# Convolution attention by query halves, with shared query rows copied on chip by GpSimd

## The chip, the cores and the metric

The kernel runs on one core of a Trainium2 chip. The metric is the device time of one launch in microseconds. The five engines of the core run their own instruction streams and wait for one another through semaphores: TensorE (PE in the profile), VectorE (DVE), ScalarE (ACT), GpSimd (POOL) and SyncE (SP). DMA transfers are issued from an engine's queue, here mostly SyncE's.

## The reference

The whole program is a convolution block with attention, then a self-attention and a mixture of experts. Only the attention beside the convolution matters here. Eight images of 32 x 32 positions, 8 heads of 8 channels:

```python
logits = jnp.einsum('bnid,bnjd->bnij', qf, kf)      # 1024 queries x 1024 keys per image and head
logits = logits + rel_w + rel_h                     # relative position terms in x and in y
weights = jax.nn.softmax(logits, axis=-1)
attn = jnp.einsum('bnij,bnjd->bnid', weights, vf)
```

## The kernel before

The function `attention` works on 16 groups (`NG`; an image and four of its heads, `HG`), each of 1024 tokens in 8 tiles of 128 (`TT`). The query operand `qf` holds, for each head and each half of the keys, a column per token and 120 rows: 64 for the relative logits in x (high and low parts), 32 for those in y (of the 16 image rows of that key half), 24 for the query channels in three parts. A 121st row (`ROW_M`) takes minus the maximum. The key operand `kf` holds one-hot rows against the relative logits, and the key channels. So one matmul over 120 or 121 rows gives complete logits. All rows but the 32 for y are the same for both key halves and are loaded twice.

Each group goes through two passes. The first pass finds the maxima: for each head and tile of 128 queries two matmuls (L664) write 128 x 1024 logits into one of two pairs of PSUM banks, `sm`, and VectorE reduces them (L644) to a column of `nmax`. For each pair of heads TensorE turns 16 such columns (L679, "turn"), VectorE casts them into `mrow` (L657), and SyncE sends them into row `ROW_M` of `qf` (`maxima`, L639, two DMAs per head). The second pass computes transposed scores, 128 keys by 512 queries, into two PSUM banks `st` (L907); ScalarE takes their exp into SBUF (L882, `probs`); TensorE multiplies by the values into `pv` (L922, `weighted`: four heads side by side in four column strips, two instructions each). ScalarE copies `pv` out (L874) and SyncE stores it (L832).

The passes are overlapped by groups: in a *period*, group n is in the second pass and group n+1 in the first, which runs four tiles ahead, so its last four tiles belong to group n+2. There are three sets of `qf`, `kf` and `va`; the third `qf` is `q_all`. In a period TensorE's order is written out: 16 double steps of two scores, one `weighted` group, two scores, and four first-pass matmuls. A score waits for the exp that frees its bank (`exp_done`). Exps and scores go by key tile, then head, then query half. The turns come at the first-pass tiles 12 and 28 of 32.

SyncE's order in a period: the loads of group n+2 (`load_queries`, L618, L620, L625, the values L820, the keys L631), once all of group n-1 is through; then the store of group n-1; then the DMAs of the maxima. Periods 1 to 12 are a hardware loop of three periods per turn. Beside this GpSimd splits the expert weights in 32 pieces (L853 to L864: load, cast, subtract, two stores), as fast as the DMAs allow.

Before the main block a start block computes the relative logits of the last four images (L783, L753, L765), stores them, loads groups 0 and 1 and makes the first pass of group 0.

## Time and profile before

| | |
|---|---|
| median of 3 runs | 2465.53 us (2460.08 to 2470.38) |
| profiled execution | 2465.86 us, span 2464.0 us, mean granted TensorE clock 0.934 |
| TensorE matmul busy | 2184.8 us (89%), 10534 instructions |
| VectorE busy | 1342.1 us (54%) |
| ScalarE busy | 1214.7 us (49%) |
| GpSimd busy | 272.7 us (11%) |
| DMA | 291.40 MB, mean 118 GB/s |
| first-pass reductions, L644 | 512, 604.0 us busy, 229.7 us idle before |
| exps, L882 | 1024, 556.6 us busy, 264.4 us idle before |

The span is that of the instructions on the slowest core; the execution's time is slightly longer. An engine's busy time is summed over its instructions. A matmul's end is modelled and matmuls overlap, so "busy" on TensorE does not mean that it runs at its peak. In a row of a timeline, the text in brackets tells how long the engine had been idle and what ended the wait; "x4" is four instructions merged into one row, whose duration runs from the first start to the last end.

### The profile page before, as it was taken

Reading aid. Unit: us, or ns where it says so; the run is one execution under the profiler, and the core shown is the slowest. Engines: PE = TensorE matmul, PEld = TensorE weight load, DVE = VectorE, ACT = ScalarE, POOL = GpSimd, SP = SyncE. Lnnn points to the kernel's source line nnn. Section 1 sums busy time; section 2 is a strip of 40 time slices with the busy share of each in tenths; the row PEclk is TensorE's granted clock in tenths of the full one; section 3 lists DMA queues with packets and bytes.
Section 4 is the critical chain, followed back from the end, with each engine's and each line's share of the span. In section 5 each row is a group of like instructions: output and inputs, shape, how many; then the busy total and the mean of one; then the engine's idle time right before and its main releaser. Section 6 shows DMA issues by size and latency. Waiting matters only on the chain. (4 is left out here: it accounts for less than half of the span.)

```text
span 2464.0 us, 32921 instructions
## 1 busy us (share of the span) xinstructions
PE 2184.8 (89%) x10534; PEld 1511.8 (61%) x10534; DVE 1342.1 (54%) x2054; ACT 1214.7 (49%) x2160; POOL 272.7 (11%) x258
## 2 busy tenths in 40 slices
PE   4999999946999999999999983888888893999997
PEld 3777888745545444454455431677777772888886
DVE  6232333124777667677777712466565652566665
ACT  2121222121467666667677771555555552566664
POOL 1000000000122222210000002212122200000000
PEclk9999999955699999999999996999999996999999
DMA  2322243396777678776567203322322114444531
GB/s 72 98 64 64 65 139 122 131 202 197 210 160 168 147 160 164 165 143 105 91 112 121 42 9 101 117 90 93 98 98 90 51 52 156 149 146 139 210 128 60
DMA packets 154696, 291.40 MB, mean 118 GB/s; under 512 B 32448, under 2 KB 94656, under 8 KB 150464
## 3 DMA queue, kind: packets, MB, share of 16 engines
q1 hardware_dynamic: 145568, 263.83, 41.6%
q0 software_dynamic: 7680, 25.17, 3.6%
q8 instruction: 75, 1.23, 0.2%
q10 hardware_dynamic: 1312, 0.67, 0.1%
q14 instruction: 61, 0.50, 0.1%
HBM read 179.69 MB, written 107.25 MB: 116 GB/s over the span
## 5 line engine op out<-in xcount | busy, mean ns | idle before, releaser
L644 DVE TENSOR_REDUCE a_nmax<-a_sm 128x1 f32<-128x1024 f32 x512 | 604.0, 1219 | 229.7 <-PE a_sm L664 229.5
L882 ACT ACTIVATE p_shared<-a_st 128x512 f32<-128x512 f32 x1024 | 556.6, 596 | 264.4 <-PE a_st L907 262.9
L922 PE MATMUL a_pv<-p_shared,a_va 128*32 128x512 f32 x2048 | 276.5, 613 | 0.9 <-ACT p_shared L882 0.9
L664 PE MATMUL a_sm<-a_kf,a_qf 120*128 120x512 f32 x704 | 218.7, 429 | 62.6 <-DMA a_kf<-kq_d 38.3
L907 PE MATMUL a_st<-a_qf,a_kf 121*128 121x512 f32 x704 | 257.5, 444 | 17.7 <-ACT p_shared L882 8.0
L907 PEld LDWEIGHTS a_st<-a_qf,a_kf 121*128 121x128 f32 x704 | 121.1, 192 | 220.4 <-ACT p_shared L882 198.3
L1797 PE MATMUL x_h_ps<-x_v_hi,x_w 128*128 128x512 f32 x512 | 180.8, 395 | 25.4 <-DVE x_v_lo L1738 25.4
L664 PEld LDWEIGHTS a_sm<-a_kf,a_qf 120*128 120x128 f32 x704 | 136.6, 204 | 100.7 <-issue 32.6
L1811 PE MATMUL x_y_ps<-x_h_hi,x_w 128*128 128x512 f32 x512 | 178.0, 389 | 0.0
L1748 DVE SCALAR_TENSOR_TENSOR x_h_lo<-x_hid,x_wts,x_h_hi 128x512 fp32r<-128x512 f32 x128 | 96.0, 750 | 138.0 <-ACT x_h_hi L1719 138.0
L1715 ACT ACTIVATE x_hid<-x_h_ps,x_b 128x512 f32<-128x512 f32 x128 | 88.4, 691 | 130.6 <-PE x_h_ps L1797 125.7
L1797 PEld LDWEIGHTS x_h_ps<-x_v_hi,x_w 128*128 128x128 f32 x512 | 97.1, 190 | 45.3 <-issue 25.5
L1382 PE MATMUL b_o_ps<-b_pT,b_v 128*128 128x256 f32 x512 | 120.7, 379 | 0.0
L1213 ACT ACTIVATE b_probs<-b_s_ps,b_nmax 128x1024 f32<-128x1024 f32 x64 | 71.3, 1113 | 95.9 <-DVE b_nmax L1303 95.9
L507 PE MATMUL c_acc<-c_y_hi,c_w_hi 128*128 128x512 f32 x288 | 117.6, 408 | 0.0
L507 PE MATMUL c_acc<-c_y_hi,c_w_hl 128*128 128x512 f32 x288 | 117.2, 407 | 0.0
L507 PE MATMUL c_acc<-c_y_lo,c_w_hi 128*128 128x512 f32 x288 | 117.1, 407 | 0.0
L507 PE MATMUL c_acc<-c_y_lo,c_w_hl 128*128 128x512 f32 x288 | 117.1, 407 | 0.0
L507 PE MATMUL c_acc<-c_y_hi,c_w_lo 128*128 128x512 f32 x288 | 117.1, 406 | 0.0
L1303 DVE TENSOR_REDUCE b_nmax<-b_s_ps 128x1 f32<-128x1024 f32 x64 | 78.4, 1224 | 69.7 <-PE b_s_ps L1367 62.9
L907 PE MATMUL a_st<-p_q_all,a_kf 121*128 121x512 f32 x320 | 112.5, 433 | 0.3 <-ACT p_shared L882 0.3
L1811 PEld LDWEIGHTS x_y_ps<-x_h_hi,x_w 128*128 128x128 f32 x512 | 96.1, 188 | 20.0
(248 smaller groups left out, 3615.2 us busy)
## 6 DMA issues: line engine op xcount, KB each, us to landing
x_w<-w_d SPq DMA_DIRECT2D x32, 1024.0 KB, 8.5
rel_d<-p_shared SPq DMA_DIRECT2D x12, 2048.0 KB, 12.2
a_qf<-rel_d SPq DMA_DIRECT2D x44, 512.0 KB
a_qf<-rel_d SPq DMA_DIRECT2D x44, 256.0 KB
p_q_all<-rel_d SPq DMA_DIRECT2D x20, 512.0 KB
a_qf<-kq_d SPq DMA_DIRECT2D x66, 128.0 KB
c_xtok<-in_x SPq DMA_DIRECT2D x8, 1024.0 KB, 5.7
va_d<-c_va SPq DMA_DIRECT2D x16, 512.0 KB, 4.8
```

The lines of the kernel that those rows point to most:

```text
L507: m = nc.tensor.matmul(image_rows(acc[u][:]), wt[:, k, :] if tap is None else wt[:, k, tap, :], y[s][:, k, rows + dy:rows + dy + H // 2, d ...
L644: nc.vector.tensor_reduce(nmax[:, h, t:t + 1], sm[k % 2][:], axis=AX.X, op=ALU.max, negate=True).then_inc(sm_read, 1)
L664: m = nc.tensor.matmul(sm[k % 2][:, cols], qf[j][0:ROW_M, h, half, t * P:(t + 1) * P], kf[j][0:ROW_M, h, cols], start=True, stop=True)
L882: nc.scalar.activation(probs[:, t % 2, h, half * HALF:(half + 1) * HALF], st[half][:], ACT.Exp).then_inc(exp_done, 1)
L907: nc.tensor.matmul(st[half][:], kf[j][0:ROW_M + 1, h, t * P:(t + 1) * P], qf[j][0:ROW_M + 1, h, 2 * t // TT, half * HALF:(half + 1) * HALF ...
L922: m = nc.tensor.matmul(pv[32 * h:32 * h + 32, cols], va[j][:, t, h, :], probs[:, t % 2, h, cols], start=t == 0, stop=t == TT - 1, skip_gro ...
L1303: nc.vector.tensor_reduce(nmax[:, k:k + 1], s_ps[:], axis=AX.X, op=ALU.max, negate=True).then_inc(max_ready, 1)
L1382: m = nc.tensor.matmul(o_ps[:], v_sb[s][:, t, :], pT[k % 2][:, t, :], start=t == 0, stop=t == TT - 1)
L1715: nc.scalar.activation(hid[k % GB][:], h_ps[k % 2][:], ACT.Gelu, bias=b1_sb[s][:, e, f:f + 1]).then_inc(hid_ready, 1)
L1748: nc.vector.scalar_tensor_tensor(h_lo[k % HB][:], hid[k % GB][:], wts[s][:, e:e + 1], bits(h_hi[k % HB][:]), ALU.mult, ALU.subtract).then_ ...
L1797: m = nc.tensor.matmul(h_ps[k % 2][:], w[s][:, e, c, part, tile(f)], v[s][:, c, half(j)], start=i == 0, stop=i == 3 * KC - 1)
L1811: m = nc.tensor.matmul(y_ps[j][c][:], w[s][:, e, 2 + f // 2, part, f % 2 * C + c * P:f % 2 * C + (c + 1) * P], h[k % HB][:], start=first a ...
```

## The change

The common rows of the queries (the x logits and the query channels, now rows 0 to 87) are loaded once per group, for key half 0; GpSimd copies them to key half 1 (`double_queries`). The y rows are still loaded per half, and lie last, before `ROW_M`. The first pass goes by halves of 512 keys in four single PSUM banks (`SB`), with a reduction per half and one minimum over the two for each pair of heads. The turns are placed after the second tile of the next head, not before its first. The second pass goes by query half first, then key tile, then head; `st` has three banks (`STB`), `pv` one bank that is copied out after each half, and `probs` four slots. TensorE's order in a period is eight batches by the string `ORDER`: s is a score, m a first-pass matmul, v a group of `weighted`. SyncE stores the second half of group n-1 ahead of the loads of group n+2, and issues the maxima of heads 0 and 1, the store of the first half, and the maxima of heads 2 and 3 after them. GpSimd handles two pieces of the expert weights per period, with the copy after the first load. The values are loaded in two DMAs.

```diff
-    ROW_W, ROW_H = (0, W), (2 * W, 2 * W + H // 2)
-    ROW_Q = 2 * W + H
-    ROW_M = ROW_Q + 3 * DH
+    ROW_W, ROW_Q = (0, W), 2 * W
+    ROW_H = (ROW_Q + 3 * DH, ROW_Q + 3 * DH + H // 2)
+    ROW_M = ROW_H[1] + H // 2
...
+        nmax_half = sb("a_nmax_half", [P, 2, HG, TT])
...
-        sm = [ctx.enter_context(nc.psum_tensor(f"a_sm{i}", [P, TOK], f32)) for i in range(2)]
+        SB = 4
+        sm = [ctx.enter_context(nc.psum_tensor(f"a_sm{i}", [P, HALF], f32)) for i in range(SB)]
...
+        DOUBLED = 2 + 3
+        VA_LOADS = 2
+        LOADS = 4 + 3 + VA_LOADS
...
-                if t == 0 and h % 2 == 0:
-                    units.append((step, "turn", 0, (h - 1) % HG, 0))
-                units.append((step, "logits", d, h, t))
-                step += 1
-            return units if whole else units + [(step, "turn", 0, HG - 1, 0)]
+                units.append((step, "logits", d, h, t, 0))
+                units.append((step + 1, "logits", d, h, t, 1))
+                if t == 1 and h % 2 == 0:
+                    units.append((step + 1, "turn", 0, (h - 1) % HG, 0, 0))
+                step += 2
+            return units if whole else units + [(step, "turn", 0, HG - 1, 0, 0)]
...
+        STEPS = 2 * TT * HG
+        NS = STEPS
+        STB = 3
+        SLOTS = 4
+        BATCH = 2 * HG
+        NB = NS // BATCH
+        ORDER = "mssmsmsvvsmsmmsmsm"
...
+            dst = bits(qf[j][:])
+            for part in range(2):
+                r = ROW_W[part]
+                sp.dma_start(dst[r:r + W, :, 0, :], rel_g[0, part]).then_inc(doubled_loaded[j], 16)
+            for row, qpart in enumerate((0, 0, 1)):
+                r = ROW_Q + DH * row
+                sp.dma_start(dst[r:r + DH, :, 0, :], kq_g[qpart, 1]).then_inc(doubled_loaded[j], 16)
             for part in range(2):
                 for half in range(2):
-                    dst = bits(qf[j][:])
-                    r = ROW_W[part]
-                    sp.dma_start(dst[r:r + W, :, half, :], rel_g[0, part]).then_inc(loaded[j], 16)
                     r = ROW_H[part]
                     sp.dma_start(dst[r:r + H // 2, :, half, :], rel_g[1, part, half * H // 2:(half + 1) * H // 2]
                                  ).then_inc(loaded[j], 16)
-            for row, qpart in enumerate((0, 0, 1)):
-                r = ROW_Q + DH * row
-                for half in range(2):
-                    sp.dma_start(bits(qf[j][:])[r:r + DH, :, half, :], kq_g[qpart, 1]).then_inc(loaded[j], 16)
+
+        def double_queries(pool, n, j):
+
+            pool.wait_ge(doubled_loaded[j], (n // BUFS + 1) * 16 * DOUBLED)
+            nc.gpsimd.tensor_copy(qf[j][0:ROW_H[0], :, 1, :], qf[j][0:ROW_H[0], :, 0, :]).then_inc(doubled, 1)
...
-        def logits_max(dve, before, k, h, t):
+        def logits_max(dve, before, k, h, t, half):
             dve.wait_ge(sm_done, before + k + 1)
-            nc.vector.tensor_reduce(nmax[:, h, t:t + 1], sm[k % 2][:], axis=AX.X, op=ALU.max, negate=True).then_inc(sm_read, 1)
+            nc.vector.tensor_reduce(nmax_half[:, half, h, t:t + 1], sm[k % SB][:], axis=AX.X, op=ALU.max, negate=True).then_inc(sm_read, 1)
+            if h % 2 and t == TT - 1 and half:
+                dve.drain()
+                nc.vector.tensor_tensor(nmax[:, h - 1:h + 1], nmax_half[:, 0, h - 1:h + 1], nmax_half[:, 1, h - 1:h + 1], ALU.min
+                                        ).then_inc(nmax_ready, 1)
...
+            if not (isinstance(before, int) and before + k < SB):
+                pe.wait_ge(sm_read, before + k + 1 - SB)
             cols = slice(half * HALF, (half + 1) * HALF)
-            m = nc.tensor.matmul(sm[k % 2][:, cols], qf[j][0:ROW_M, h, half, t * P:(t + 1) * P],
-                                 kf[j][0:ROW_M, h, cols], start=True, stop=True)
-            if half == 1:
-                m.then_inc(sm_done, 1)
-
-        def first_pass(pe, n, j, whole, s, half, va_after=0):
-
-            for k, (step, what, d, h, t) in enumerate(first_pass_of[whole]):
-                if step == s and what == "logits":
+            nc.tensor.matmul(sm[k % SB][:], qf[j][0:ROW_M, h, half, t * P:(t + 1) * P],
+                             kf[j][0:ROW_M, h, cols], start=True, stop=True).then_inc(sm_done, 1)
...
-        probs = bits(shared[:])
+        probs = bits(shared[:]).rearrange("p a h n -> p (a h n)").rearrange("p (t h n) -> p t h n", t=SLOTS, h=HG)
         out = sb("a_out", [P, TOK])
-        st = [ctx.enter_context(nc.psum_tensor(f"a_st{i}", [P, HALF], f32)) for i in range(2)]
-        pv = ctx.enter_context(nc.psum_tensor("a_pv", [P, TOK], f32))
+        st = [ctx.enter_context(nc.psum_tensor(f"a_st{i}", [P, HALF], f32)) for i in range(STB)]
+        pv = ctx.enter_context(nc.psum_tensor("a_pv", [P, HALF], f32))
...
                 def period(n, j, more, ahead):
+                    if not (isinstance(n, int) and n == 0):
+                        store(n - 1, 1)
                     if ahead:
                         load(n + 2, (j + 2) % BUFS)
-                    if not (isinstance(n, int) and n == 0):
-                        store(n - 1)
                     if more:
-                        maxima(sp, n + 1, (j + 1) % BUFS, ahead)
-
-                def store(n):
-                    sp.wait_ge(out_ready, n * 2 + 4)
-                    sp.dma_start(att_d.rearrange("b g p n -> (b g) p n")[n], out[:]).then_inc(out_stored, 16)
-
-                sp.sem_inc(out_stored, 16)
+                        maxima(sp, n + 1, (j + 1) % BUFS, ahead, 0)
+                    store(n, 0)
+                    if more:
+                        maxima(sp, n + 1, (j + 1) % BUFS, ahead, 2)
...
+                for n in range(NG):
+                    load_weights(2 * n)
+                    if n + 2 < NG:
+                        double_queries(pool, n + 2, (n + 2) % BUFS)
+                    split_weights(2 * n)
+                    load_weights(2 * n + 1)
+                    split_weights(2 * n + 1)
...
                     for u in range(NS):
-                        t, h, half = u // (2 * HG), u // 2 % HG, u % 2
                         act.wait_ge(st_done, n * NS + u + 1)
-                        if h == half == 0:
-                            act.wait_ge(pv_done, n * 2 * TT + 2 * t + 2)
-                        nc.scalar.activation(probs[:, t % 2, h, half * HALF:(half + 1) * HALF], st[half][:], ACT.Exp
-                                             ).then_inc(exp_done, 1)
-                        if u in (3, 7) and not (isinstance(n, int) and n == 0):
-                            copy_out(n - 1, u // 4)
+                        if u % BATCH == 0:
+                            act.wait_ge(pv_done, n * 2 * TT + 2 * (u // BATCH) + 2)
+                        nc.scalar.activation(probs[:, u // HG % SLOTS, u % HG], st[(j + u) % STB][:], ACT.Exp).then_inc(exp_done, 1)
+                        if u == BATCH - 1 and not (isinstance(n, int) and n == 0):
+                            copy_out(n - 1, 1)
+                        if u == NS // 2 + BATCH - 1:
+                            copy_out(n, 0)
...
+                def weighted(n, j, w):
+
+                    half, t = w // TT, w % TT
+                    pe.wait_ge(exp_done, n * NS + HG * (w + 1) + STB)
+                    if w == 0:
                         pe.wait_ge(loaded[j], times_loaded(n, j))
                     if t == 0:
-                        pe.wait_ge(out_ready, n * 2 + half + 1)
-                    cols = slice(half * HALF, (half + 1) * HALF)
+                        pe.wait_ge(out_ready, n * 2 + half + 2)
...
                 def period(n, j, more, ahead):
-                    for s in range(0, STEPS, 2):
-                        t, h = s // HG, s % HG
-                        for half in range(2):
-                            scores(n, j, s, half)
-                        if t:
-                            weighted(n, j, t - 1, h // 2)
-                        elif not (isinstance(n, int) and n == 0):
-                            weighted(n - 1, (j - 1) % BUFS, TT - 1, h // 2)
-                        for half in range(2):
-                            scores(n, j, s + 1, half)
-                        if more:
-                            for step in (s, s + 1):
-                                for half in range(2):
-                                    first_pass(pe, n + 1, (j + 1) % BUFS, ahead, step, half)
-
-                pe.sem_inc(exp_done, 2)
+                    for i in range(NB):
+                        place = dict.fromkeys("smv", 0)
+                        for what in ORDER:
+                            k = place[what]
+                            place[what] += 1
+                            if what == "s":
+                                scores(n, j, i * BATCH + k)
+                            elif what == "m" and more:
+                                first_pass(pe, n + 1, (j + 1) % BUFS, ahead, i * BATCH + k)
+                            elif what == "v" and i:
+                                weighted(n, j, 2 * (i - 1) + k)
+                            elif what == "v" and not (isinstance(n, int) and n == 0):
+                                weighted(n - 1, (j - 1) % BUFS, 2 * (NB - 1) + k)
```

`scores`, the start block and the waits of the other engines follow the new counts. A score waits for `exp_done` at `n * NS + u + 1`, which starts at 3, that is for the exp three scores back.

## Rows read from the trace of the kernel before

**Rows 1.** Windows view: us, busy by engine (instructions), clock, DMA share, GB/s
```profile
494.00:646.00 152.00, 90.14 (x330) 77.04 (x330) 72.54 (x74) 29.76 (x36) 5.28 (x8) 0.50 0.74 193
646.00:1483.00 837.00, 806.46 (x4054) 394.00 (x4054) 568.81 (x506) 570.48 (x1057) 116.58 (x160) 0.98 0.63 126
```

**Rows 2.** Timeline, one double step: start us, us, engine, line, count, [idle before]
```profile
927.45 0.73 PE L907 MATMUL a_st<-p_q_all,a_kf 121*128 121x512 f32 x2
...
927.99 1.09 ACT L882 ACTIVATE p_shared<-a_st 128x512 f32<-128x512 f32 x2 [0.53 <-PE a_st L907]
928.02 1.09 PE L664 MATMUL a_sm<-a_kf,a_qf 120*128 120x512 f32 x4
928.69 2.36 DVE L644 TENSOR_REDUCE a_nmax<-a_sm 128x1 f32<-128x1024 f32 x2 [0.74 <-PE a_sm L664]
...
928.95 0.68 PE L907 MATMUL a_st<-p_q_all,a_kf 121*128 121x512 f32 x2
929.13 0.19 PEld L907 LDWEIGHTS a_st<-p_q_all,a_kf 121*128 121x128 f32 x1 [0.22 <-ACT p_shared L882]
...
929.56 1.06 PE L922 MATMUL a_pv<-p_shared,a_va 128*32 128x512 f32 x8
...
930.56 0.73 PE L907 MATMUL a_st<-p_q_all,a_kf 121*128 121x512 f32 x2
```

**Rows 3.** Timeline in the last group, which has no first pass
```profile
1441.26 0.73 PE L907 MATMUL a_st<-a_qf,a_kf 121*128 121x512 f32 x2
...
1444.36 0.73 PE L907 MATMUL a_st<-a_qf,a_kf 121*128 121x512 f32 x2
...
1480.10 1.92 PE L922 MATMUL a_pv<-p_shared,a_va 128*32 128x512 f32 x16 [0.94 <-ACT p_shared L882]
```

**Rows 4.** Timeline of VectorE, casts of the maxima
```profile
669.23 0.28 DVE L657 CAST a_mrow<-a_sm 16x128 fp32r<-16x128 f32 x1 [0.45 <-PE a_sm L679]
...
1351.35 0.28 DVE L657 CAST a_mrow<-a_sm 16x128 fp32r<-16x128 f32 x1 [0.45 <-PE a_sm L679]
...
1401.59 0.28 DVE L657 CAST a_mrow<-a_sm 16x128 fp32r<-16x128 f32 x1 [0.45 <-PE a_sm L679]
```

**Rows 5.** Timeline around a load wait and the loop's return
```profile
847.74 1.21 PE L664 MATMUL a_sm<-a_kf,p_q_all 120*128 120x512 f32 x4 [1.43 <-DMA a_kf<-kq_d]
...
855.25 1.22 PE L907 MATMUL a_st<-a_qf,a_kf 121*128 121x512 f32 x2 [3.25 <-issue]
...
856.40 1.94 PE L922 MATMUL a_pv<-p_shared,a_va 128*32 128x512 f32 x8
...
864.89 1.06 PE L922 MATMUL a_pv<-p_shared,a_va 128*32 128x512 f32 x8
```

**Rows 6.** Timeline, DMA issues: first load of a group; four maxima
```profile
805.14 0.68 SPq L618 DMA_DIRECT2D p_q_all<-rel_d  x1
...
904.73 2.69 SPq L639 DMA_DIRECT2D p_q_all<-a_mrow  x4
```

**Rows 7.** Waits view, 650 to 1480: us in total, times, longest
```profile
PE a_sm L664 <- DMA a_kf<-kq_d: 11.3, 6, 3.5
```

**Rows 8.** Timeline of VectorE in the start of the phase
```profile
545.30 1.22 DVE L644 TENSOR_REDUCE a_nmax<-a_sm 128x1 f32<-128x1024 f32 x1 [29.17 <-PE a_sm L664]
547.53 0.69 DVE L765 TENSOR_TENSOR p_shared<-a_rel,p_shared 128x512 fp32r<-128x512 f32 x1 [1.01 <-ACT p_shared L753]
```

**Rows 9.** View of DMA issues: count, KB each, median us to landing
```profile
kq_d<-c_kq_hi SPq DMA_DIRECT2D x32, 128.0 KB, 2.1
...
att_d<-a_out SPq DMA_DIRECT2D x1, 512.0 KB, 4.0
...
c_cb<-in_L_conv_conv_b SPq DMA_DIRECT2D x1, 0.5 KB, 5.2
```

**Rows 10.** Timeline of GpSimd
```profile
906.01 0.61 POOL L859 CAST p_bd_hi<-a_w_st 128x512 fp32r<-128x512 f32 x1 [16.69 <-DMA a_w_st<-in_L_ffn_W]
```

**Rows 11.** Waits view, 494 to 646
```profile
ACT a_hl L753 <- DMA rel_d<-a_hl: 25.7, 1, 25.7
```

157 lines of the change are left out of this document (87 added, 70 removed).

## The prediction

> **What bounds the kernel now.** I read the busy times by stage first. In the query/key attention stage (646 to 1483 us) TensorE counts as busy nearly throughout and VectorE and ScalarE for two thirds; in the start of the phase (494 to 646) TensorE runs at half clock while the DMA engines move 193 GB/s [rows 1]. "Busy" is weak here, since matmuls overlap, so I read the order of time next. A double step takes 3.11 us: two score matmuls (to the next start 0.57), four first-pass matmuls (0.93), two scores (0.61; a weight load is held 0.22 by an exp), one group of eight P·V matmuls (1.00) [rows 2]. Then the next scores start. The last group is the test, since it has no first pass: there the four first-pass matmuls are gone, and a double step still takes 3.10 us (1441.26 to 1444.36) [rows 3]. So the bound is not TensorE's work but a ring: score, exp on one of only two score banks, second score pair held until the exps free the banks, P·V behind them in TensorE's order, and only then the next scores: 0.54 to the first exp, 1.09 for two exps, about 0.48 to the P·V start, 0.99 for it, 3.10 in all.
>
> A period (one group, 16 double steps, two turns of the maxima) undisturbed is 50.24 us (casts at 1351.35 and 1401.59); over the 14 periods from 669.23 the mean is 52.3, so 29.0 us are lost in them [rows 4]. I see two causes. One is a load that arrives late: TensorE idles 1.43 us at 847.74 for keys whose group's loads began at 805.14 [rows 5, 6]; six such waits sum to 11.3 us [rows 7]. The other has no releaser and comes at the period where the hardware loop of three periods returns (three times): scores start at 855.25 after 3.25 us, and the next P·V group takes 1.94 us in place of 1.06, which is TensorE at half clock (1.2 of 2.4 GHz). From the first-pass matmuls at 847.74 to the P·V group at 864.89 lie 17.15 us where 0.93+0.61 and three double steps make 10.87, so one return costs up to 6.3 us [rows 5].
>
> **Part by part.**
> *Score banks 2 to 3, first-pass banks two of 1024 to four of 512, P·V by query halves, fixed order over 8 scores, 8 first-pass matmuls, 2 P·V groups.* The number of matmuls of each kind stays. The ring opens: at "mssmsmsvvsmsmmsmsm" score u needs the exp of score u-3. I walk one batch with 0.23 us per score or first-pass matmul (0.93 for four), 0.39 from a score's matmul to its exp, 0.545 per exp: the third score follows without a wait, the fourth (1.3 us in) needs the first exp (1.16), the four after P·V find free banks, and the eight exps end 0.6 us into the next batch, whose first scores need only exps 6 to 8. TensorE therefore becomes its own bound: two half batches of 0.57+0.93+0.45 each are 3.90 (0.45 is two scores at 0.225 with no exp to wait for); two P·V groups in a row take 0.86+1.00 (sixteen last 1.92 with the last one's own tail [rows 3], eight 1.06 [rows 2]), and one of two load exposures after P·V goes (0.12). That is 5.64; the walk with 0.225 per matmul gives 5.45; I take 5.6, 44.8 us for eight batches. Add two transposes (0.5 with their loads) and two places where the copy out of P·V delays an exp by 0.5 of which 0.3 reaches TensorE: 45.9.
>
> *Maxima by halves.* 64 reductions of 512 replace 32 of 1024. Two of 1024 last 2.36 us [rows 2], a single one 1.22 [rows 8], so the second starts 1.14 after the first. A VectorE operation of 512 columns from PSUM lasts 0.69 [rows 8]; from the 1024 form, less 512 columns at 1.04 ns, I also get 0.69. If successive ones overlap as now, their spacing is 0.69 less 0.08, 0.61: 4.9 us per batch, under TensorE's 5.6; without overlap 5.5, just under. Four banks hold 2.4 us of reductions through the P·V pair. The two minima and two casts of a period are under 0.3 each [rows 4]. I count 0.
> The Trainium skill, page "VectorE: DVE Perf Modes", section "The TRN2 errata", says an instruction pays a fixed term (about 150 cycles measured for one copy) and so speaks against halving tiles; charged fully, 64 reductions take an estimated 44 us per period, which is the third rival below.
>
> *The second turn of the maxima gets later.* Now its casts come four of 32 tiles before the end and scores of heads 2 and 3 are needed 3.1 us into the next period. After the change the transpose stands behind first-pass matmul 59 of 64, 3.9 us into the last batch; VectorE finishes that tile's reduction at 4.7, the cast at 5.0, and SyncE then issues four DMAs of the maxima in 2.69 us [rows 6]. The next period (from 5.75) wants heads 0, 1, 2, 3 in its first four scores, head 2 at 6.6 and head 3 at 7.1. With a landing 2.1 us after issue (the fastest small store [rows 9]), head 2 is there at 7.7 and head 3 at 9.0. So 2.0 us of new wait per period, in front of P·V and everything behind on TensorE. Bounds: 0 if landing is faster than any row shows; 4.0 (a store on an idle queue) gives 3.9; 5.2 (a 0.5 KB load at the start) gives 5.1 [rows 9]. I take 2.1: nothing else should be in the queue by then. Period: 45.9+2.1 = 48.0, against 50.2.
> The Trainium skill, "DMA: Bandwidth & Descriptors", section "Anatomy of one DMA", gives about 2.0 us fixed cost, most of it the write receipt; by it the wait is the same 2 us, and it also says a small size does not shorten it, which speaks against this edit. No row shows the landing of a maxima DMA itself.
>
> *Loads.* Per group now 4.63 MB (8 of 512 or 256 KB, six and three of 128 KB, values 512 KB); afterwards 3.25 MB. At 4.63 MB in the 42.6 us from 805.14 to 847.74 [rows 5, 6] (109 GB/s with the expert weights beside) 3.25 MB take 30 us. But SyncE now first waits for the copy out of the second half, at the end of the first batch and behind the new wait, so loads begin about 9 us into the period, not 3.5. Landing 39 to 41, needed at 42.4 (last batch): in time by 1 to 3 us. The weights go at two pieces per period, not some 3.5, which lightens the queue; their last pieces still end within the last period, hidden. The waits of 11.3 us go, with the half clock behind them: of the 29.0 us I leave 16 for three loop returns (5.3 each) and drop 13.
>
> *The copy on GpSimd.* 88 partitions by 4096. A 512-column cast there lasts 0.61 us [rows 10], so at most 8 x 0.61 = 4.9 us. Its inputs are loaded first (1.38 MB, 13 us), so it ends about 27 us into the period of 48: hidden by 15 us; the split of weights queued behind it is nobody's wait in this phase. Cost 0; if it were 20 us the first pass would wait.
>
> *Last group.* Without first pass a batch is 0.45+0.45 for the scores before the P·V pair, 1.86, 0.9, plus where ScalarE idles across the pair: by the walk 5.3, 42.4 against 49.6.
>
> *Start of the phase.* ScalarE waits 25.7 us for a store of relative logits [rows 11] that stands in SyncE's queue behind the loads of groups 0 and 1. These shrink by 2.75 MB; at 193 GB/s [rows 1] 14 us. Reductions of half size cost about 0.1 us more per 1024 columns where VectorE leads (33 of them, 3 us). Net 11; from 0 to 18.
>
> **Sum.** Before: 15 x 50.2 + 49.6 + 29.0 + about 4 for the first period = 836, which is the stage. After: 15 x 48.0 + 42.4 + 16 + 4 = 782. Gain 54, plus 11: 65. The profiled execution took 2465.86 us for a span of 2464.0 and lies on the median 2465.53: 2401, say 2400. What follows the phase is unchanged.
>
> **Rivals.**
> A, the wait for maxima isn't there (landing under 1 us, or slack in the ring hides it): period 46, 15 x 2.1 = 31 less, 2370. Speaks for it: no row shows these landings. Against: every landing read is 2 us or more. Chance 0.15.
> B, VectorE leads: no overlap of 512 reductions; in the stretch where seven first-pass matmuls come within 3 us the fourth bank is freed 0.3 us late, each batch: 8 x 0.25 = 2 us per period, 2430. Against: the pair of 2.36. Chance 0.14.
> C, loads later than their use, because they begin 5.5 us later in the period: 3 us of wait and clock loss in 15 periods, 45: 2445. Chance 0.08.
> D, slower: the maxima land 5.2 us after issue, as the small load did. The wait is then 5.1 us in two pieces, and TensorE falls to half clock after them, as at 855; that P·V group alone lost 0.88, a return 3 us beyond its idle time. Period 45.9+5.1+3 = 54.0: 15 x 3.8 = 57 more, less 7 (last group), 13 and 11: 2490. It decides from about 6.4 us of loss per period. Against: the queue is empty then. Chance 0.06.
> E, the exchange is neutral (ring gain eaten by a wait of 5 us): 2460. Chance 0.04.
>
> **Numbers.** Forecast 2400 with 0.53. Under 0.5% (12 us) a measurement of this kernel cannot tell from no change. The range runs from A's 2370 less the early loads' 10 to C's 2445: 2360 to 2445. Faster 0.53+0.15+0.14+0.06 of C = 0.88; same 0.05 (E and part of C); slower 0.07 (D and part of C).
>
> **What would show it.** The double step's two-bank ring gone: ScalarE waiting in other places, batch starts 5.6 us apart (5.4 to 5.7). Cast to cast of one kind 48 us. A wait of scores for the maxima once a period, 2 us. The two VectorE reductions 1.22 to 1.3 us per pair. No first-pass wait on loads of keys. The stage 646 to 1483 shortened to 782; the start from 152 to 141. It would be wrong if batches took over 5.9 us, or if the wait at the period's start passed 4 us.

## The result

The changed kernel takes 2449.1 us (median of 19 runs, 2436.7 to 2462.4) beside 2467.2 for the kernel before on the same chips (19 runs): a ratio of 0.9923, 95% interval 0.9906 to 0.9939. That is 18 us faster where 65 were forecast, and 4 us above the range. The profiled execution has a span of 2444.8 us (before 2464.0).

The two stages of [rows 1], in the windows view of the changed kernel:

```profile
494.00:646.00 152.00, 108.75 (x409) 89.05 (x410) 87.61 (x133) 43.06 (x60) 13.26 (x11) 0.54 0.78 204
646.00:1483.00 837.00, 771.08 (x3977) 402.75 (x3975) 583.07 (x993) 548.04 (x1035) 166.50 (x176) 0.97 0.59 100
```

In the start TensorE gets 409 matmuls done by 646 us instead of 330: work begins earlier (that window already holds some of the first period's matmuls in the changed kernel). To see the main stage apart from that, I use the casts of the maxima as the clock, as in [rows 4]. The same cast stands 17.9 us earlier than there, at 651.35 for 669.23, and 14 periods later at 1386.89:

```profile
651.35 0.27 DVE L681 CAST a_mrow<-a_sm 16x128 fp32r<-16x128 f32 x1
...
704.73 0.27 DVE L681 CAST a_mrow<-a_sm 16x128 fp32r<-16x128 f32 x1
...
754.96 0.27 DVE L681 CAST a_mrow<-a_sm 16x128 fp32r<-16x128 f32 x1
...
1386.89 0.27 DVE L681 CAST a_mrow<-a_sm 16x128 fp32r<-16x128 f32 x1
```

So the mean period is 735.54/14 = 52.5 us, 0.2 more than the 52.3 of before, and the least one (704.73 to 754.96) is 50.2, what it was. From that last cast to the last P·V the changed kernel takes 77.0 us, before 79.8. So the 18 us are the start's: the 14 periods lose 3 us and the last group gains 3. The forecast had periods of 48.0 and some 16 us of loss in 14 of them, 49.1 in the mean. It is the 3.4 us a period between 49.1 and 52.5 that has to be found.

One batch (8 scores, 8 first-pass matmuls, 16 P·V matmuls) in TensorE's timeline of the changed kernel:

```profile
713.63 0.50 PE L955 MATMUL a_st<-a_qf,a_kf 121*128 121x512 f32 x1
714.07 1.92 PE L968 MATMUL a_pv<-p_shared,a_va 128*32 128x512 f32 x16
715.92 0.51 PE L955 MATMUL a_st<-a_qf,a_kf 121*128 121x512 f32 x1
716.26 0.39 PE L688 MATMUL a_sm<-a_kf,p_q_all 120*128 120x512 f32 x1
716.50 0.40 PE L955 MATMUL a_st<-a_qf,a_kf 121*128 121x512 f32 x1
...
719.57 0.47 PE L955 MATMUL a_st<-a_qf,a_kf 121*128 121x512 f32 x1
719.97 1.93 PE L968 MATMUL a_pv<-p_shared,a_va 128*32 128x512 f32 x16
```

P·V starts at 714.07 and 719.97: 5.90 us, for the forecast's 5.6. No row has idle time in brackets (the view prints none below 0.15 us), so the batch is mainly TensorE's own stream. But the ring of [rows 2] is not fully open. The last score's weight load and the exps beside it:

```profile
718.89 2.07 ACT L930 ACTIVATE p_shared<-a_st 128x512 f32<-128x512 f32 x4 [0.18 <-PE a_st L955]
...
719.54 0.19 PEld L955 LDWEIGHTS a_st<-a_qf,a_kf 121*128 121x128 f32 x1
```

The first of these four exps ends at 719.49, 0.60 us after its start, and it is the one three scores back: the weight load of the last score before P·V begins 0.05 us behind it, 0.12 us after the load before it ended. In 103 of the 117 batches between 650 and 1420 us this weight load begins 0.05 us after that exp. Single matmuls start 0.23 us apart (716.26 to 716.50), the first one after P·V takes 0.34 and the last score before it 0.40. VectorE does its eight reductions behind it with a pause left, and at the end of a period this happens:

```profile
716.70 4.88 DVE L663 TENSOR_REDUCE a_nmax_half<-a_sm 128x1 f32<-128x512 f32 x8 [1.23 <-PE a_sm L688]
...
728.00 0.56 POOL L907 DMA_DIRECT2D w_d<-p_bd_hi  x1 [0.30 <-POOL p_bd_lo L904]
...
728.29 0.27 PE L705 MATMUL a_sm<-a_ident,a_nmax 128*16 128x128 f32 x1
...
729.09 0.54 POOL L893 DMA_DIRECT2D a_w_st<-in_L_ffn_W  x1
729.11 0.27 DVE L681 CAST a_mrow<-a_sm 16x128 fp32r<-16x128 f32 x1
...
729.40 2.70 SPq L658 DMA_DIRECT2D p_q_all<-a_mrow  x4
...
732.93 0.47 PE L955 MATMUL a_st<-p_q_all,a_kf 121*128 121x512 f32 x1 [1.32 <-DMA p_q_all<-a_mrow]
```

Eight reductions take 4.88 us (0.60 apart), under the 5.90. The transpose of the second turn at 728.29 leads to a cast at 729.11 and four DMAs of the maxima from 729.40; the scores that need them start at 732.93 after 1.32 us of waiting. Beside them stand two rows of GpSimd's queue at the same moment (its store of a weight half at 728.00 and its next load at 729.09): these matter below.

The longest waits of TensorE in the stage (columns: us in total, times, longest):

```profile
PE a_st L955 <- DMA a_qf<-a_mrow: 12.2, 8, 2.6
PE a_sm L688 <- issue: 10.8, 3, 3.7
PE a_st L955 <- DMA p_q_all<-a_mrow: 7.3, 5, 1.9
PE a_sm L688 <- DVE a_nmax_half L663: 6.8, 30, 0.9
PE a_sm L688 <- DMA a_kf<-kq_d: 4.0, 4, 1.4
```

The maxima are now waited for, 19.5 us in 13 waits at 11 places; the keys still, 4.0 in place of 11.3 [rows 7]; and the loop's three returns ("issue", 10.8). TensorE ran at half clock for some 3 to 5 us after all three returns and after four of the eleven places (near 681, 784, 1049 and 1262), and after none of the four waits for keys. The wait of 1.58 us at 783.41 and the return at 837.13, each with the P·V pair behind it (1.92 us otherwise) and the clock of the stretch:

```profile
783.41 0.47 PE L955 MATMUL a_st<-a_qf,a_kf 121*128 121x512 f32 x1 [1.58 <-DMA a_qf<-a_mrow]
...
785.13 3.17 PE L968 MATMUL a_pv<-p_shared,a_va 128*32 128x512 f32 x16
...
837.13 0.79 PE L688 MATMUL a_sm<-a_kf,p_q_all 120*128 120x512 f32 x1 [3.65 <-issue]
...
840.41 2.84 PE L968 MATMUL a_pv<-p_shared,a_va 128*32 128x512 f32 x16
```

```profile
785.00:789.00 4.00, 4.00 (x20) 1.27 (x20) 0.00 (x0) 0.82 (x2) 0.00 (x0) 0.66 0.01 2
837.00:842.00 5.00, 4.87 (x15) 2.62 (x19) 2.08 (x3) 2.28 (x4) 0.00 (x0) 0.50 0.03 7
```

Granted clock 0.66 and 0.50. SyncE's part of a period, in its timeline:

```profile
739.13 0.38 SPq L871 DMA_DIRECT2D att_d<-a_out  x1
739.81 1.47 SPq L631 DMA_DIRECT2D a_qf<-rel_d  x2
...
746.98 1.15 SPq L650 DMA_DIRECT2D a_kf<-kq_d  x3
```

The loads begin at 739.81, directly behind the store of the second half at 739.13, as forecast: 9 us into the period, whose first score starts at 730.75.

### The profile page after: what moved, and what is told of

The parts are those of the page before. It is cut to its first block and busy times, and to the rows that moved or that the text cites. A ratio compares the mean times of both kernels' runs of the same rounds, so it can differ in the third digit from the quotient of the medians.

```text
span 2444.8 us, 34315 instructions
## 1 busy us (share of the span) xinstructions
PE 2167.8 (89%) x10534; PEld 1531.7 (63%) x10534; DVE 1370.7 (56%) x2598; ACT 1204.2 (49%) x2160; POOL 329.9 (13%) x274
## 5 line engine op out<-in xcount | busy, mean ns | idle before, releaser
L663 DVE TENSOR_REDUCE a_nmax_half<-a_sm 128x1 f32<-128x512 f32 x1024 | 633.4, 682 | 204.6 <-PE a_sm L688 204.2
L930 ACT ACTIVATE p_shared<-a_st 128x512 f32<-128x512 f32 x1024 | 547.0, 604 | 275.8 <-PE a_st L955 266.6
L688 PE MATMUL a_sm<-a_kf,a_qf 120*128 120x512 f32 x704 | 277.9, 438 | 48.7 <-DMA a_kf<-kq_d 27.8
L955 PE MATMUL a_st<-a_qf,a_kf 121*128 121x512 f32 x704 | 288.4, 433 | 16.0 <-DMA a_qf<-a_mrow 12.2
L968 PE MATMUL a_pv<-p_shared,a_va 128*32 128x512 f32 x2048 | 258.0, 623 | 0.0
L955 PEld LDWEIGHTS a_st<-a_qf,a_kf 121*128 121x128 f32 x704 | 135.0, 193 | 142.3 <-ACT p_shared L930 100.5
L955 PE MATMUL a_st<-p_q_all,a_kf 121*128 121x512 f32 x320 | 128.8, 424 | 7.9 <-DMA p_q_all<-a_mrow 7.3
L688 PE MATMUL a_sm<-a_kf,p_q_all 120*128 120x512 f32 x320 | 121.1, 410 | 14.3 <-issue 10.8
L968 PEld LDWEIGHTS a_pv<-p_shared,a_va 128*32 128x32 f32 x2048 | 54.8, 112 | 116.4 <-issue 89.2
```

Source lines behind the costliest of these rows:

```text
L663: nc.vector.tensor_reduce(nmax_half[:, half, h, t:t + 1], sm[k % SB][:], axis=AX.X, op=ALU.max, negate=True).then_inc(sm_read, 1)
L688: nc.tensor.matmul(sm[k % SB][:], qf[j][0:ROW_M, h, half, t * P:(t + 1) * P], kf[j][0:ROW_M, h, cols], start=True, stop=True).then_inc(sm_ ...
L930: nc.scalar.activation(probs[:, u // HG % SLOTS, u % HG], st[(j + u) % STB][:], ACT.Exp).then_inc(exp_done, 1)
L955: nc.tensor.matmul(st[(j + u) % STB][:], kf[j][0:ROW_M + 1, h, t * P:(t + 1) * P], qf[j][0:ROW_M + 1, h, 2 * t // TT, half * HALF:(half + ...
L968: m = nc.tensor.matmul(pv[32 * h:32 * h + 32, :], va[j][:, t, h, :], probs[:, w % SLOTS, h], start=t == 0, stop=t == TT - 1, skip_group_ch ...
```

## The experiments

The theory at the start: the smaller load and the rearrangement by halves are two changes, the first gives what is gained, and the second exchanges the ring for TensorE's stream plus waits. Rivals were VectorE as the bound (B), the maxima's wait, and late loads (C).

**1. The smaller load and the copy alone,** in the kernel before: its order, two score banks and its P·V stay. The weights go at two pieces a period, as in the changed kernel.

```
 # kernel before, with load_queries, double_queries and the
+# weights' two pieces per period of the changed kernel
-        ROW_W, ROW_H = (0, W), (2 * W, 2 * W + H // 2)
+        ROW_W, ROW_Q = (0, W), 2 * W
```

> The kernel before with the loads alone changed: common query rows loaded once and copied by GpSimd, expert weights two pieces per period; both passes and their order stay as before. Theory 1 (the rearrangement by halves is worth nothing by itself, all of the gain is the smaller load): the start of the phase gets 18 us shorter, as in the changed kernel (block start 646 to 628), and the key waits of the first pass (11.3 us plus half clock) go: 2467 - 18 - 13 = 2436, below the changed kernel's 2449. Theory 2 (the rearrangement brings most of it): only the start gains, period mean stays 52.3: 2449 or above.

2437.95 us, ratio 0.9871 (0.9843 to 0.9899) against the kernel before: faster than the whole change. Its first cast of a period stands at 651.73, where the changed kernel has it too, so the start's gain comes with this part. No wait of TensorE for keys is left, and the mean period is 51.5: 50.1 to 50.5, and 55.1 to 56.4 at the three returns. No run separates the smaller load from the slower weights in the periods; for the start, run 2 does, which has these weights with the full load.

**2. The rearrangement alone:** the changed kernel, with both halves of the rows loaded.

```
-                sp.dma_start(dst[r:r + W, :, 0, :], ...).then_inc(doubled_loaded[j], 16)
+                for half in range(2):
+                    sp.dma_start(dst[r:r + W, :, half, :], ...).then_inc(loaded[j], 16)
```

> The changed kernel, but with both key halves' query rows loaded from memory again (19 DMAs less one, no copy on GpSimd). Theory 1: the start's 18 us are lost, and with 4.63 MB beginning some 9 us into the period instead of 3.5 the keys arrive late in every period: 2449 + 18 + 3 to 6 us in each of 13 periods = 2500 to 2540, slower than before. Theory 2: the load has slack, 2467.

2680.88 us, ratio 1.085 (1.0821 to 1.0879). The direction was right, the size far off: 15 us a period in the mean (67.5 for 52.5) where 3 to 6 were expected. The first cast stands at 676.44, 25 us later than with the smaller load, so the start's gain is not the weights'. The waits view has the cause:

```profile
PE a_sm L683 <- DMA a_kf<-kq_d: 188.4, 14, 16.2
```

188 us, up to 16.2 each. Without the smaller load the loads are the bound; the forecast had not asked what the new order does by itself. That the loads have become so close a bound made me look at them again after the next two.

**3. The maxima of key half 0 first,** each half with a semaphore of its own, so that the first four scores wait only for their half.

```
+            for half in range(2):
+                for h in (first, first + 1):
+                    ... .then_inc(max_loaded[half][h], 16)
```

> The changed kernel; of the four DMAs of maxima per turn, the two rows of key half 0 go first and have semaphores of their own, so that the first four scores of a period wait for two issues and not four (1.35 us less of 2.69). Theory 1 (the late maxima, and the half clock that the wait brings in some periods, eat the gain): the 1.3 to 1.9 us waits before the third score shrink to 0.6 at most, the waits of scores for the maxima rows fall from 19.5 us in total to under 6, and two or three half-clock stretches of 3.4 us go: 2449 - 14 - 8 = 2427 (2420 to 2435). Theory 2 (TensorE's batch of 5.90 us is all, the wait is hidden by VectorE's or ScalarE's lag): 2445 to 2449.

2454.72 us (2448 to 2470), ratio to the kernel before 0.9936 (0.9917 to 0.9955), beside 0.9923 for the changed kernel: no gain, mean period 52.8. The waits for the maxima fell from 19.5 to 15.3 us, those for keys rose from 4.0 to 10.3 and the returns from 10.8 to 13.5. Expected were waits under 6 us, so the run did not take them away, and it says only that sending key half 0 first is no cure.

**4. Reductions over 256 of the 512 columns** (half of the maxima's columns is left out), which takes load from VectorE only.

```
-            ... sm[k % SB][:], axis=AX.X, op=ALU.max, negate=True)
+            ... sm[k % SB][:, 0:256], axis=AX.X, op=ALU.max, negate=True)
```

> The changed kernel with every first-pass reduction over 256 of its 512 columns (the maximum of the other half is left out; the softmax is shifted by another number). VectorE's eight reductions per batch fall from 4.88 to some 2.7 us. Theory 1 (TensorE's issue bounds the batch): batches stay at 5.9 less at most 0.05, only the turn's 0.6 us bubble goes, about 1 us a period: 2435. Rival B of the prediction (VectorE holds the first-pass banks): batches fall to 5.6 or below, 2410.

2448.46 us, one run. A clean batch still takes 5.88 us, for 5.90: VectorE is not what holds the stage, and rival B, which expected 0.25 to 0.3 us a batch, is out. The waits view says where the time went instead:

```profile
PE a_sm L688 <- DMA a_kf<-kq_d: 18.6, 11, 7.5
...
PE a_sm L688 <- DVE a_nmax_half L663: 0.8, 2, 0.6
```

TensorE's waits for reductions went from 6.8 to 0.8 us, and those for keys from 4.0 to 18.6. In runs 3 and 4 alike, what is shortened in front comes back as a wait for keys: the loads are a second bound just behind the first.

**5. The loads ahead of the store.** Both wait for the last P·V of the group before; the store also for the copy out.

```
-                    if not (isinstance(n, int) and n == 0):
-                        store(n - 1, 1)
                     if ahead:
                         load(n + 2, (j + 2) % BUFS)
+                    if not (isinstance(n, int) and n == 0):
+                        store(n - 1, 1)
```

> The changed kernel with SyncE's loads for the group after next put ahead of its store of the second half. Both wait for the same P.V (ends near 735.7 in the period that begins at 731); the store also waits for the copy-out behind the batch's exponentials, so the loads start near 736 instead of 739.8. Theory 1 (late loads are a second bound that takes back what the TensorE stream gives): no first-pass waits for keys are left (4.0 us in the changed kernel), fewer windows at half clock, and the mean period falls from 52.5 towards 51.5; 2430 to 2442. Theory 2 (the loads land in time but for a few, the losses are turn, maxima and loop returns): within 0.3% of the changed kernel, 2442 to 2456. Theory 3 (contention): loads that begin while the maxima land delay the scores, 2455 or more.

2429.91 us (4 runs), ratio 0.9844 (0.981 to 0.9877): some 19 us less than the changed kernel (by the two medians, and by the two ratios), by two lines moved. Its SyncE and its waits:

```profile
725.71 2.69 SPq L658 DMA_DIRECT2D p_q_all<-a_mrow  x4
732.19 1.47 SPq L631 DMA_DIRECT2D a_qf<-rel_d  x2
...
740.77 0.39 SPq L871 DMA_DIRECT2D att_d<-a_out  x1
```

```profile
PE a_sm L688 <- issue: 9.0, 3, 3.4
PE a_st L955 <- DMA a_qf<-a_mrow: 6.4, 7, 1.2
...
PE a_st L955 <- DMA p_q_all<-a_mrow: 3.6, 6, 0.7
```

The loads start 6.5 us behind the issue of the maxima (725.71), not 10.4 (729.40 to 739.81). No wait for keys is left. The waits for the maxima fell too, from 19.5 to 10.0 us. None of them is followed by half clock here. Mean period 51.1; outside the returns 50.0 to 50.8. Theory 1 holds, and 1.4 us of the missing 3.4 is found: in 15 periods some 9.5 us of waits for the maxima, 4 for keys, 2 at the returns, and the four stretches at half clock, each 1.3 us or more (an estimate from the P·V pair at 785.13, 3.17 us for 1.92).

**6. Still earlier: rows at the scores' end,** only the values behind P·V.

```
+                    if late:
+                        sp.wait_ge(st_done, (n - 2) * NS)
                     load_queries(sp, n, j)
```

> As the run before, but query and key rows are loaded as soon as the last score of the group that held the buffers is done (near 732 in that period, 7.6 us earlier than in the changed kernel), and only the values wait for P.V. Theory 1: keys are never late and the DMA engines have the whole period; mean period 50.5 to 51.5, 2418 to 2438. Theory 2: within 0.3% of the changed kernel. Theory 3: the row loads queue up with the four maxima DMAs (2.7 us from cast to landing): if these are still under way at the scores' end they take longer, the maxima waits grow from 1.3 us a period, 2455 or more.

2446.08 us, ratio 0.9912 (0.9881 to 0.9942): the gain of run 5 is gone. The timelines of VectorE and GpSimd give a reason that neither theory had:

```profile
749.23 3.60 POOL L644 CAST a_qf<-a_qf 88x4096 fp32r<-88x4096 f32 x1 [28.16 <-DMA a_qf<-kq_d]
...
750.66 2.20 DVE L666 TENSOR_TENSOR a_nmax<-a_nmax_half 128x16 f32<-128x16 f32 x1
...
752.78 2.47 DVE L663 TENSOR_REDUCE a_nmax_half<-a_sm 128x1 f32<-128x512 f32 x4
```

The minimum of the two half maxima, 0.18 us otherwise, starts at 750.66 and ends within 0.05 us of GpSimd's copy (749.23 + 3.60 = 752.83). The longest of the 32 took 3.36 us, and each of the nine that took over 0.2 us ends some 0.03 us after the copy does. The earlier rows had moved the copy onto the minimum, and the turn behind it waited.

**7. The same with the copy in four pieces,** one for each head.

```
-            nc.gpsimd.tensor_copy(qf[j][0:ROW_H[0], :, 1, :], qf[j][0:ROW_H[0], :, 0, :])
+            for h in range(HG):
+                last = nc.gpsimd.tensor_copy(qf[j][0:ROW_H[0], h, 1, :], qf[j][0:ROW_H[0], h, 0, :])
```

> The kernel that loads the rows at the scores' end, with GpSimd's copy cut into four, one for each head. In that kernel VectorE's 128x16 minimum, 0.18 us otherwise, took 2.20 us at 750.66 and ended when GpSimd's 3.60 us copy (from 749.23) did, and up to 3.36 us elsewhere; the turn behind it waited. Theory 1 (the long copy holds VectorE's SBUF-to-SBUF operation, and that is why the earliest loads gained nothing): with pieces of 0.9 us the minimum takes at most some 1.1 us, the waits of the turn for VectorE (6.2 us) and half the periods above 52 go; 2420 to 2435. Rival (the early loads cost by their DMA traffic beside the maxima, and the minimum is a bystander): 2440 to 2450 as before.

2434.72 us, ratio 0.9849 (0.9817 to 0.9882): 11 us back (16 by the ratios, whose intervals just touch), and the turn's waits for reductions, 6.2 us in run 6, no longer stand in the view. The longest minimum is now 1.04 us, as long as a piece. The overlap is shown by the rows; its price of 11 us is likely from this run, and not measured closely. It is no better than run 5, since the maxima are waited for 12.6 us.

**8. First pass six tiles ahead,** on run 6.

```
-        AHEAD = TT // 2
+        AHEAD = 6
```

> The run before with the first pass six query tiles ahead instead of four: the last turn comes four logits matmuls (about 1.5 us of the stream) earlier, so the maxima land before the scores want them; the next keys are wanted 1.5 us earlier too. Theory 1: with the loads early this is free, the 1.3 us wait at each group's start goes, and the half clock behind it: 15 to 25 us below b2, 2400 to 2418, and the period is the batches' 47.2 plus turn and copies, 48.5 to 50. Rival (the least period of 50.2 has another cause than the maxima, such as the 5.90 us batches being stretched by copies and turns): same as b2.

2439.41 us, ratio 0.9881 (0.9852 to 0.991). The waits for the maxima are gone altogether, as expected, but of the 15 to 25 us only 7 came: TensorE waits for VectorE's reductions 24.0 us instead (7.3 in run 6), and the periods with a return are 57.4 to 58.2.

**9. Two score banks** in the changed kernel.

```
-        STB = 3
+        STB = 2
 # scores and exps take bank u % STB in place of (j + u) % STB
```

> The changed kernel with two score banks in place of three (the first pass keeps four banks). If the rearranged order is what takes the ring of score, exponential and score out of the way, nothing changes: 2445 to 2455. If the third bank does it, the batch goes from 5.90 to the ring's 6.20 to 6.22 (two double steps of 3.10 to 3.11 in the kernel before): 8 x 15 x 0.31 = 37 us, 2475 to 2490.

2491.2 us, ratio 1.009 (1.0062 to 1.0119). P·V to P·V:

```profile
717.55 1.92 PE L968 MATMUL a_pv<-p_shared,a_va 128*32 128x512 f32 x16
...
723.97 1.93 PE L968 MATMUL a_pv<-p_shared,a_va 128*32 128x512 f32 x16
```

6.42 us, a little over the ring's 6.20, and a mean period of 54.8. So without the third bank the ring is the bound again; the new order on two banks is worse than the old.

**10. A first pass of 256 columns** on run 5 (matmuls and reductions; a part of the maxima is left out).

```
-            nc.tensor.matmul(sm[k % SB][:], qf[j][0:ROW_M, ...
+            nc.tensor.matmul(sm[k % SB][:, 0:256], qf[j][0:ROW_M, ...
```

> The kernel with the loads ahead of the store, with the first pass's matmuls and reductions over 256 of the 512 keys of a half (a part of the maxima is left out). Theory: TensorE's stream is what sets the batch, so it falls from 5.90 us by eight first-pass matmuls of half the columns (8 x 0.107 = 0.85 us) to about 5.1 to 5.3 unless ScalarE's eight exponentials of 0.53 us with their hand-over bound it first; main stage 15 x 8 x 0.6 = 70 us shorter, 2350 to 2370. If the loads bound the period from behind (11 DMA-engine seconds of 0.63 x 50 us = 32 us of full use a period), the gain shows as waits for keys instead.

2398.04 us, one run; a miss of 30 us. Clean batches fell to 5.43 us (P·V at 686.59 and 692.02 in the timeline), so TensorE's stream sets most of the 5.90. But it was relieved of 0.85 us and only 0.47 came: 5.43 is also what a batch takes in the last group, which has no first pass at all. By the rows that is the ring with three banks (in 108 of 122 batches the last score's weight load begins 0.05 us after the exp three scores back), only 0.5 us under the 5.90. The rest was taken back by waits:

```profile
PE a_st L955 <- DMA a_qf<-a_mrow: 17.5, 10, 4.0
PE a_st L955 <- ACT p_shared L930: 13.6, 41, 0.5
...
PE a_sm L688 <- DMA a_kf<-kq_d: 11.0, 7, 5.6
```

Keys 11.0 us again, and 28.3 for the maxima. 12 of the 32 us were gained before the first full period.

**11. The weights moved behind the last copy,** in the changed kernel.

```
                 for n in range(NG):
-                    load_weights(2 * n)
                     if n + 2 < NG:
                         double_queries(pool, n + 2, (n + 2) % BUFS)
+                for n in range(NG):
+                    load_weights(2 * n)
```

> The changed kernel with GpSimd's part of the experts' weights (two loads, splits and stores a period) moved behind its last copy, which lengthens the end of the stage by some 28 x 7 us and is of no interest; read are the periods of the groups before that. Theory 1 (the weights' stores, put behind the copy that the late rows hold up, run beside the maxima's small transfers, and the weights' traffic keeps the rows late): the maxima's waits fall from 1.3 us a period to 0.7 or less as in the kernel with the earlier loads, the waits for keys vanish, and the undisturbed periods are 50.2. Rival (the late loads alone do it): waits as in the changed kernel, mean period 52.5.

2558.48 us, of which only the periods are read: mean 51.9 for 52.5. The waits for the maxima fell from 19.5 to 10.5 us, close to run 5's 10.0; those for keys stayed (4.2). So theory 1 is right on the maxima and wrong on the keys. In the changed kernel GpSimd issues its store of weights at 728.00, 1.4 us before the maxima at 729.40. In run 5 the copy starts at 701.12 in place of 709.03 and that store at 721.56, 4.1 us before the maxima at 725.71. The rows of the other periods agree, those with a return left out. Where GpSimd's last DMA is issued 1.3 us or more before the first of the maxima, or none is near (runs 5, 11 and 12), the score of head 2 starts 2.55 to 2.9 us after that issue. In the changed kernel GpSimd's last one is issued within 0.7 us of it in nine of ten periods, and that score starts 3.3 to 4.8 us after. So the chain is: a later load delays the copy, the copy the weights queued behind it, and these run beside the maxima. The link from weights to maxima is shown by this run, the link before it only by the rows.

**12. Run 5 with the loop written out.**

```
-            with eng.Fori(1, (steps - 1) * BUFS + 2, BUFS) as n:
-                for i in range(BUFS):
-                    period(n + i, (1 + i) % BUFS, True, True)
-            for n in range(1 + steps * BUFS, NG):
+            for n in range(1, NG):
                 period(n, n % BUFS, n < NG - 1, n + 2 < NG)
```

> The kernel with the loads ahead of the store, with its hardware loop of three periods written out, so that no engine returns. Theory: the periods at the loop's returns (55.1, 53.3 and 53.6 against 50.2 to 50.6) fall to the others' length, 11 us in all: 2416 to 2422. Rival: the instruction stream is three to four times as long and its fetching costs as much everywhere, or the periods are long for the half clock that anything can set off: 2428 to 2445.

2407.89 us (2404.9 to 2410.4), ratio 0.9731 (0.97 to 0.9762): the best of all, 61.5 us under the kernel before on the same chip (2469.4). Every period from cast to cast is now 49.8 to 50.1. All of TensorE's waits on DMAs and on "issue" in the stage:

```profile
PE a_st L952 <- DMA a_qf<-a_mrow: 9.0, 18, 0.7
...
PE a_st L952 <- DMA p_q_all<-a_mrow: 4.8, 10, 0.6
```

"issue" is gone, and the maxima cost 13.8 us in 28 waits of 0.7 at most. Expected were 11 us and 22 came (by the ratios 28, with some 11 either way): not only the three long periods, but up to 0.8 us in the others too. Run 5's trace is that of its fastest execution (2420.8 us) and run 12's that of its slowest (2410.4), so the traces differ by 10 us only. The rows show where the other periods gain. Inside the hardware loop the first exp of a batch starts 0.51 us after its score (median), written out 0.43, and a clean batch takes 5.83 us for 5.90, 0.6 us in eight. In the changed kernel's own trace the periods outside its loop have 0.44 and 5.83:

```profile
1332.15 0.19 PEld L955 LDWEIGHTS a_st<-a_qf,a_kf 121*128 121x128 f32 x1
...
1332.26 0.40 PE L955 MATMUL a_st<-a_qf,a_kf 121*128 121x512 f32 x1
1332.59 1.92 PE L968 MATMUL a_pv<-p_shared,a_va 128*32 128x512 f32 x16
```

Here the last score's weight load comes 0.11 us before its matmul and not 0.03, and from that score to P·V it is 0.33 us and not 0.40. That first exp is the one which the last score waits for, and the only one of its batch for which ScalarE also waits for P·V (`pv_done`). What in the loop delays it is not shown.

**13 and 14. The copy-only kernel and the changed kernel with the loop written out.**

> The copy-only kernel (one load and GpSimd's copy, order and banks as before) with its hardware loop written out. Theory (the rearrangement by halves is worth 8 x 0.3 us a batch only in that the two-bank ring's 6.20 becomes 5.90; the loop's returns cost both kernels alike): its periods become 50.3 throughout, so the stage ends 14 periods x 0.5 us later than that of the unrolled kernel by halves with early loads (49.8); 2414 to 2424, against 2408 there. Rival (the rearrangement is worth nothing once loads and loop are out of the way): 2402 to 2412.

> The changed kernel, its loads where it has them, with the hardware loop written out. Theory 1 (late loads and loop returns are separate costs that add): 20 to 22 us faster than the changed kernel, 2425 to 2430, with first-pass waits for keys and maxima waits as there. Rival (a return makes the loads of its period late and the half clock follows; without returns the late loads cost little): 2408 to 2416, near the unrolled kernel with the early loads.

2418.93 us (0.9804, 0.9762 to 0.9846) and 2425.47 (0.9836, 0.979 to 0.9881), both inside the theory's range. Written out, the copy-only kernel's periods are 50.2 to 50.4; run 12's are 49.8. So with loads and loop out of the way the rearrangement by halves is worth some 11 us (ratios 0.9804 and 0.9731, whose intervals just touch; by them it is 18), and as it was made it cost 11 (0.9923 against 0.9871). The changed kernel's loop and its late loads are separate costs: 24 us (2449.1 to 2425.5) and 18 us (2425.5 to 2407.9), near the 22 and 19 that they are worth in the other order (by the ratios 21 and 26 here, 28 and 19 there).

**15. Run 12 with the copy in four and six tiles ahead.**

> The unrolled kernel with the loads ahead of the store, with GpSimd's copy in four pieces and the first pass six tiles ahead. Its periods of 49.8 hold 0.9 us of waits for the maxima (13.8 us in 15), which this takes away; with six tiles ahead VectorE was late for the turns before (24.0 us of waits for its reductions, periods of 50.6). Theory (the turns wait for VectorE instead, the wait only changes its name): periods 49.8 to 50.6, 2405 to 2420. Rival (VectorE was late there because of the long copy and the loop): 48.8 to 49.2, 2393 to 2402.

2414.36 us, ratio 0.9786 (0.9743 to 0.9829). The wait only changes its name, as the theory said: none for the maxima, 25.5 and 6.5 us for VectorE, mean period 50.8. Run 12 stays the best.

## Why the prediction was wrong, step by step

- *Bound before.* Right: with two banks the ring holds the new order too (run 9). A third opens it but for some 0.1 us a batch, and leaves it at most 0.5 us behind (5.43).
- *Batch 5.6 us.* Wrong by 0.30, and this is the largest term: 8 x 0.30 = 2.4 us a period, 36 us in 15. The step that failed is "0.45 is two scores at 0.225 with no exp to wait for". There is an exp to wait for: the last score's weight load is held by the exp three scores back, as in [rows 2], and this score takes 0.40 up to P·V (719.57 to 719.97). Where the exp costs nothing (the two weight loads 0.04 us apart, as elsewhere) it takes 0.33 (1332.26 to 1332.59), still 0.1 more than the 0.23 of the others. So of 0.17 us some 0.07 is the hold and 0.10 the step to P·V; the rest of the 0.30 is mostly the 0.233 of each matmul for 0.225 and the rounding down. The number was in reach: in [rows 2] the pair before P·V takes 0.61, and the forecast put all of the excess down to the held weight load (0.22). The walk had that exp done 1.16 us into the batch, with 0.39 us from score to exp and 0.545 for the exp, and the score that needs it at 1.3. In the trace these are 0.51 and 0.60, and the exp ends 1.36 us into the batch (718.12 to 719.49). Of the 36 us the loop has some 8, 0.07 a batch (run 12).
- *Turns and copies, 1.1 us.* 1.7: in 725.86 to 733.81 (P·V to P·V over a turn) are 7.95 us, less 5.90 and 1.32 of wait, 0.73 for one turn where 0.25 stood; copies 0.1 to 0.2 each.
- *Wait for the maxima 2.1 us.* Mechanism and place right, size 1.3 in the changed kernel and 0.9 undisturbed (run 12). Here the forecast was too high by 1.2, which hid half of the batch's error; that is luck. The landing itself was about right: in run 12 the score of head 3 starts 3.90 us after the first of four DMAs, and the fourth is issued some 2.0 us after it (2.69 us for four), which leaves an estimated 1.9 us for the 2.1. What was off is when the scores want the maxima: the period's first score starts 1.64 us after the cast (729.11 to 730.75), where the walk had about 1.0.
  By the Trainium skill, page "DMA: Bandwidth & Descriptors", section "Anatomy of one DMA", a DMA pays a fixed 2.0 us or so whatever its size. That section has it for DMAs issued by GpSimd, and these are SyncE's; the estimated 1.9 us agrees with it.
- *Undisturbed period 48.0.* The best one of the changed kernel is 50.2: 47.2 for eight batches, 1.7 and 1.3. Written out it is 49.8 (run 12): 46.6 for eight batches of 5.83, 2.3 for turns and copies, 0.9 for the wait. That is 1.8 us off the forecast, 27 us over 15 periods; the rest of the way to 50.2 is counted with the loop.
- *Loads in time by 1 to 3 us; 16 us left for returns.* The second failed step, 1.4 us a period, about 20 us in all (run 5; run 14 against 12 gives 18). The forecast had the loads begin some 9 us into the period and saw it, gave the case of late loads a chance of 0.08 (rival C, 2445), and took 1 to 3 us of margin as enough. It was not: keys were waited for (4.0 us), and the weights' DMAs ran beside the maxima, by the rows because the later copy pushed them there. A margin smaller than the spread of its own estimate is no cover. The loop was sized about right in total, 51.1 of run 5 less 49.8 of run 12 is 1.3 us a period for 16/14 = 1.1, but in part by luck: the three periods with a return cost some 11 us and not 16, and the rest is the 0.07 us a batch that the forecast did not have.
- *VectorE.* Right: 0.60 apart, 4.88 a batch. The Trainium skill, page "VectorE: DVE Perf Modes", section "The TRN2 errata", has a fixed term for each instruction, measured for a copy; these are reductions from PSUM. The rows show 0.68 us for one of 512 columns and 0.60 from one to the next: at the 1.04 ns a column of the forecast some 0.15 us is fixed, and half of that is hidden. The rival built on it (B, which the forecast calls its third) was wrong (run 4).
- *GpSimd's copy.* 3.60 us, under the bound of 4.9, and hidden from its readers. That GpSimd can hold VectorE was not in the forecast. In the changed kernel the copy never did so, but its split of the weights did three times: minima of 0.25, 0.33 and 0.91 us end 0.03 us after a cast or a subtraction of the weights. The Trainium skill, page "SBUF — State Buffer", section "Who interferes with whom", states it: GpSimd and VectorE share a pair of ports, a VectorE operation with two inputs in SBUF contends with a GpSimd one that reads SBUF, and a reduction on trn2 never does. Run 6 agrees in both halves: the minimum took 2.20 and 3.36 us, and the 36 reductions that lie within a copy took 0.69 us at most, 0.68 in the middle. By that rule the forecast should have asked where in the period the copy falls.
- *Last group 5.3 a batch.* 5.43 to 5.44:

```profile
1435.03 1.92 PE L968 MATMUL a_pv<-p_shared,a_va 128*32 128x512 f32 x16
...
1440.47 1.92 PE L968 MATMUL a_pv<-p_shared,a_va 128*32 128x512 f32 x16
```

- *Start, 11 us (0 to 18).* 17.9, at the upper end. ScalarE's wait for the store fell from 25.7 [rows 11] to 17.1 us; by the first cast 12.6 us were gained (596.27 for 608.89), the rest in the first full period.

From the last of these casts to the last P·V are 77.0 us (1386.89 to 1463.9), before 79.8 (1401.59 to 1481.4): 2.8 gained where the last group was to give 7.

The sum: 3.4 us x 15 periods = 51, less 7 for the start, and 4 for the last group: 48 of the 49 us between 2400 and 2449.

## What to carry to other kernels

When one bound is taken away, write down the next two with their margins. A margin of 1 to 3 us on a load that the same change starts 5 us later is a cost and not a cover. Before sizing a new order of matmuls, read the spacing at each switch of kind from the trace (here 0.33 to 0.40 and 0.34 beside 0.23), and multiply it by the number of switches. Look at the weight loads too before calling a ring open: the timeline of the matmuls alone does not show a hold of 0.1 us. A change of two parts should be tried by parts: here one part gave the gain, and the other showed its own only after two lines of the queue had changed places and the loop was written out.
